# A decoder layer with a state-space mixer: local outputs and states in two phases over both row halves, later gate tiles in other PSUM banks, carried factors made on GpSimd

## The reference, cut to what matters

```python
zxbcdt = X @ W_in.T
z, xBC, dt = jnp.split(zxbcdt, [D_INNER, D_INNER + CONV_DIM], axis=-1)
dt = jax.nn.softplus(dt + dt_bias)
...                                   # causal convolution of 4 taps over xBC, then silu
x, Bm, Cm = jnp.split(xBC, [D_INNER, D_INNER + D_STATE], axis=-1)
dA = jnp.exp(dt * A)                  # 16 heads of 64 channels, 64 states
dBx = jnp.einsum('blh,bln,blhp->blhpn', dt, Bm, xh)
def step(h, inp):
    h = h * dA_t[:, :, None, None] + dBx_t
    y = jnp.einsum('bhpn,bn->bhp', h, C_t)
...
y = ys.transpose(1, 0, 2, 3) + D[None, None, :, None] * xh
y = y * jax.nn.silu(z)
y = y * jax.lax.rsqrt(jnp.mean(y * y, axis=-1, keepdims=True) + EPS) * norm_w
return y @ W_out.T
```

## Time and profile before

| | us |
|---|---|
| median of 3 runs | 2098.51 (2094.14 to 2098.99) |
| the profiled execution | 2095.91 |
| its span | 2094.1 |
| the mixer, from the start to the first matmul of the next stage | 911 |
| one sequence of it, the sixth (582.20 to 689.47) | 107.27 |
| its four groups and its tail | 17.05, 17.69, 17.09, 12.55, 42.88 |
| TensorE busy, of the span | 1952.8 (93%) |

### The profile page before, as it was taken

The page is one execution under the profiler, slowest core; times in us unless marked ns, Lnnn a source line. Parts: engine busy times, 40 slices in busy tenths (PEclk is TensorE's granted clock), DMA queues, the critical chain, the costliest instruction groups (busy, mean ns, idle before and its releaser), DMA issues. The chain is left out here.

```text
span 2094.1 us, 38522 instructions
## 1 busy us (share of the span) xinstructions
PE 1952.8 (93%) x12588; PEld 1310.0 (63%) x12588; DVE 1453.7 (69%) x2889; ACT 1223.2 (58%) x3068; POOL 410.5 (20%) x629
## 2 busy tenths in 40 slices
PE   7899999999999999858999999999999999889988
PEld 5667676767676767535565566555565655478853
DVE  8978787878787878525757676757676766555438
ACT  4435353444444453316878787877878686646514
POOL 1110111111111010230122222221313122200006
PEclk9999999999999999889999999999999999999999
DMA  7121222222221212232334333332323332641156
GB/s 217 49 76 63 61 79 60 79 50 89 50 89 42 97 34 85 81 114 62 102 82 122 82 111 83 106 92 90 109 88 100 104 87 77 192 162 61 61 178 265
DMA packets 120044, 200.60 MB, mean 96 GB/s; under 512 B 23088, under 2 KB 44592, under 8 KB 119600
## 3 DMA queue, kind: packets, MB, share of 16 engines
q1 hardware_dynamic: 110640, 179.20, 28.2%
q0 software_dynamic: 9216, 18.89, 3.5%
HBM read 117.27 MB, written 29.88 MB: 70 GB/s over the span
## 5 line engine op out<-in xcount | busy, mean ns | idle before, releaser
L1777 ACT ACTIVATE a_shared<-a_shared,a_mx 128x512 f32<-128x512 f32 x512 | 341.4, 670 | 62.8 <-DVE a_mx L1838 62.7
L1770 ACT ACTIVATE a_probs<-a_scores 128x512 f32<-128x512 f32 x512 | 292.3, 605 | 92.0 <-PE a_scores L1980 89.7
L1838 DVE TENSOR_REDUCE a_mx<-a_shared 128x1 f32<-128x512 f32 x512 | 318.8, 683 | 17.4 <-PE a_shared L1964 16.4
L1980 PE MATMUL a_scores<-a_qs,a_ks 98*128 98x512 f32 x512 | 217.7, 433 | 23.5 <-ACT a_probs L1770 20.0
L1964 PE MATMUL a_shared<-a_ks,a_qs 96*128 96x512 f32 x512 | 215.8, 432 | 24.6 <-ACT a_shared L1777 14.9
L939 PE MATMUL m_proj<-m_xt_hi,link 128*128 128x512 f32 x544 | 223.7, 411 | 6.8 <-DVE m_acc L652 6.8
L1094 PE MATMUL m_outp<-m_wout,m_g 128*128 128x512 f32 x512 | 226.0, 600 | 2.7 <-issue 2.7
L940 PE MATMUL m_proj<-m_xt_lo,link 128*128 128x512 f32 x544 | 214.7, 395 | 0.0
L941 PE MATMUL m_proj<-m_xt_hi,link 128*128 128x512 f32 x544 | 213.5, 392 | 0.0
L467 ACT ACTIVATE m_acc<-m_proj,m_cb,m_cw 128x512 f32<-128x512 f32 x72 | 58.1, 817 | 257.8 <-PE m_proj L941 257.6
L1938 PE MATMUL a_shared<-link 128*128 128x512 f32 x768 | 189.7, 400 | 18.6 <-POOL a_ks L1700 15.8
(11 more groups left out here) (267 smaller groups left out, 3456.4 us busy)
## 6 DMA issues: line engine op xcount, KB each, us to landing
m_dec<-step_decay SPq DMA_DIRECT2D x64, 256.0 KB, 4.1
a_qs<-link SPq DMA_DIRECT2D x256, 64.0 KB, 2.5
m_ce<-run_decay SPq DMA_DIRECT2D x128, 112.0 KB, 3.6
a_ks<-a_k_hi POOLq DMA_DIRECT2D x192, 64.0 KB, 2.5
e_x<-x SPq DMA_DIRECT2D x11, 1024.0 KB, 5.7
m_xt_in<-x_t_in SPq DMA_DIRECT2D x8, 1024.0 KB, 7.4
m_x_tok<-x_in SPq DMA_DIRECT2D x8, 1024.0 KB, 5.7
x<-m_x_tok SPq DMA_DIRECT2D x32, 256.0 KB, 2.2
```

The lines of the kernel that those rows point to most:

```text
L1770: act.activation(probs[:, n % 2, h, :], scores[t.score_bank(n, h)][:, :], ACT.Exp, scale=-1.0).then_inc(exp_ready, 1)
L1777: act.activation(scored[:, :], scored[:, :], ACT.Exp, scale=-1.0, bias=mx[:, i % 2, j, h:h + 1], accum_out=den[:, i, j, h:h + 1]).then_inc ...
L1838: dve.tensor_reduce(mx[:, i % 2, j, h:h + 1], bank(what)[:, :], AX.X, ALU.min).then_inc(mx_ready, 1)
L1980: pe.matmul(scores[t.score_bank(n, h)][:, :], ks[0:STACK + 2, t.slot(i), h, j * P:(j + 1) * P], qs[0:STACK + 2, t.slot(i), h, :], start=Tr ...
```

## The change

Five things change, all in the mixer.

1. The local outputs are written in two phases. In phase 0 row half 0 writes into y bank 0 and row half 1 into y bank 1, in phase 1 the other way round, and the products of both row halves alternate. The number of products is the same (32 of the program for each group; a product of two fp32 operands shows as two records in the trace). Phase 0 stands where the local outputs stood, phase 1 behind the first part of the added states.
2. The added states are split likewise: chunks 0, 5 and 2, then 4, 1, 6 and 3. The semaphore `half_done` stands in place of `even_done`.
3. From group 1 on the first gate tile goes to `outp` 1 and the second to `proj` 0, and the second y bank of group 3 is `outp` 1. With this go other waits: the first gate tile no longer waits for a convolution, the local outputs of group 3 wait for only one of the two skip terms, and each half of `xdt` is waited for by itself.
4. The carried factors are made by GpSimd, one group ahead of its sums of squares, and no longer by VectorE.
5. The decays of group 3 are made half in group 0 and half in group 1 (two heads each), and ahead of the states. In the first sequence they stay where they were.

```diff
+        def z_bank(gr, j):
+            return proj[j] if gr == 0 else (outp[1], proj[0])[j]
+
+        def y_bank(gr, j):
+            return outp[1] if gr + 1 == NG and j else yp[j]
...
+        STATE_PHASES = [(0, 5, 2), (4, 1, 6, 3)]
...
+            def carried_factors(b, gr):
+                loaded = value(pool, at(b, 64 * NG // 2, 64 * (gr // 2 + 1)))
...
+                pool.wait_ge(ce_in[gr % 2], loaded)
+                pool.tensor_tensor(ce[:, gr % 2], ce[:, gr % 2],
+                                   ct[:, Q:SEQ].unsqueeze(1).to_broadcast([P, 2, SEQ - Q]), ALU.mult
+                                   ).then_inc(ce_ready, 1)
...
                 for gr in range(NG):
-                    sum_squares(b, first, gr)
+                    carried_factors(b, gr)
+                    if gr:
+                        sum_squares(b, first, gr - 1)
+                sum_squares(b, first, NG - 1)
...
-            def local_decays(b, gr):
+            def local_decays(b, gr, heads=range(HG)):
...
-            def carried_factors(b, gr):
-                dve.wait_ge(ce_in[gr % 2], at(b, 64 * NG // 2, 64 * (gr // 2 + 1)))
-                dve.tensor_tensor(ce[:, gr % 2], ce[:, gr % 2],
...
-                        carried_factors(b, gr)
+                    if not first and gr < 2:
+                        local_decays(b, NG - 1, range(2 * gr, 2 * gr + 2))
                     states(b, first, gr)
                     if first and gr + 1 < NG:
                         local_decays(b, 1 + gr)
-                    elif gr == 0:
-                        local_decays(b, NG - 1)
...
-                elif (n - 2) % 4 < 2:
-                    pe.wait_ge(z_ready, at(b, XT_TILES, 2 * ((n - 2) // 4 - 1) + (n - 2) % 4 + 1))
+                elif part >= 2 and gr == 0:
+                    pe.wait_ge(conv_read, at(b, 9, part))
+                elif part == 2:
+                    if gr >= 2:
+                        pe.wait_ge(z_ready, at(b, XT_TILES, 2 * gr - 1))
+                    elif not first:
+                        pe.wait_ge(out_read, at(b, TT, 0))
+                elif part == 3:
+                    pe.wait_ge(conv_read, at(b, 9, 2 * gr + 2))
+                elif part == 0:
+                    pe.wait_ge(z_ready, at(b, XT_TILES, 1 if gr == 1 else 2 * gr))
...
-                for c in (0, 2, 4, 6, 1, 3, 5):
+                if phase == 0:
...
+                    pe.wait_ge(xw_ready, weighted)
+                else:
...
+                    pe.wait_ge(half_done, halves)
+                for c in STATE_PHASES[phase]:
...
-                for r in range(2):
-                    half = slice(r * Q, (r + 1) * Q)
-                    for j in range(2):
...
+                for k in range(CH):
+                    if phase == 0 and k % 2 == 0:
+                        met(pe, w_used, 1)
+                        pe.wait_ge(xdt_ready, scaled[k // 2])
+                    for h in range(2):
+                        for r in range(2):
+                            j, half = r ^ phase, slice(r * Q, (r + 1) * Q)
+                            ins = pe.matmul(y_bank(gr, j)[h * HP:(h + 1) * HP, k * P + r * Q:k * P + (r + 1) * Q],
+                                            xdt[half, k, 2 * j + h, :], dec[half, gr, 2 * j + h, k * Q:(k + 1) * Q],
+                                            start=(phase == 0 and k == 0), stop=False, skip_group_check=True)
...
-                    local_outputs(b, first, gr)
+                    local_outputs(b, first, gr, 0)
                     if gr + 1 < NG:
                         z_tile(b, first, gr + 1, 0)
                     elif more:
                         dt_proj(b + 1, False)
-                    added_states(b, first, gr)
+                    added_states(b, gr, 0)
+                    local_outputs(b, first, gr, 1)
+                    added_states(b, gr, 1)
```

100 lines of the change are left out of this document (49 added, 51 removed).

## The result

| | before | after | ratio |
|---|---|---|---|
| median us (range, runs) | 2098.75 (2094.14 to 2100.26, 4) | 2136.08 (2134.93 to 2137.55, 4) | 1.0184 [1.0168, 1.0200] |
| span of the profiled execution | 2094.1 | 2135.8 | |

A forecast was written before the change was run, and what follows sets the result against it. TensorE was taken to set the mixer's pace, VectorE close behind. Six middle sequences (-9.9), the last (-1.65) and the first (-2) sum to -13.6 us, -11.8 with the clock: median 2086 us, range 2075 to 2101.

The forecast's parts named there:

- the one on GpSimd: GpSimd's new carried-factor products: 2.2 us each, fitting its idle time, costing VectorE 0.4 us in the second group.
- A forecast of +0.5: First group of a middle sequence: early decays delay the states, so it ends 0.5 us later; bounds 0.3 to 0.7.
- The second group: Second group: 17.69 to 17.1 us, gain 0.6; scans go first at the port after the last sum, costing 0.4.
- GpSimd is first at the port: Rival, second group: carried factors start before the scans, which stand 2.2 us, 1.8 more in seven groups: 2099; chance 0.15.
- a rival of 0.10: Clock rival: half clock after the first group's wait, 1.7 us per x-tile stretch, last groups too: 2101 to 2113; chance 0.10.
- the forecast's two: Last groups: half clock expected in two more of seven, +1.8 us in all; bounds -2.6 to +3.6.
- the first sequence: First sequence: VectorE loses carried factors but GpSimd blocks its casts and splits; 2 us shorter, bounds -4 to 0.
- a forecast gain of 11.8: Whole kernel: all sequences sum to -13.6 us, -11.8 with the clock's loss in last groups.
- The two blocks: TensorE's local outputs and states per group: blocks of 0.71 and 1.46 us, 2.17 in place of 3.53.
- the row halves' overlap: TensorE's blocks: row halves run side by side; the rival without overlap keeps 3.53 us, total 2098, chance 0.08.
- The last group: Last group of a sequence: only the second block counts, 0.15 us less; the step-size tile still waits for the split.
- The sum: Whole kernel: profiled execution 2095.91 becomes 2084 us; median said as 2086.

The follow-up runs named there:

- e2: The kernel before with only the carried factors moved to GpSimd, in the changed kernel's order: 2138.0 us, 1.0183 of before.
- e9: The changed kernel with only GpSimd's first two products moved, behind the scaled x and group 0's first state: 2116.0 us, 1.0097 of before.
- e3: The changed kernel with GpSimd's products delayed: first until x is scaled, second until group 0's first state, third until group 3's decays: 2090.8 us, 0.9965 of before.
- e6: The changed kernel with each GpSimd product for the carried factors cut into four of 224 elements, same queue place: 2111.1 us, 1.0046 of before.
- e7: The changed kernel with only GpSimd's third product moved, behind the decays of group 3: 2114.5 us, 1.0057 of before.
- e5: The changed kernel with nine unused matmuls before the second group's carried outputs, from the second sequence on: 2143.4 us, 1.0198 of before.
- e8: e3 with the early decays moved between the two convolutions and no wait for GpSimd's third product: 2063.6 us, 0.9813 of before.
- e10: e8 with the carried factors on VectorE, ahead of the states: 2086.9 us, 0.9951 of before.
- e4: The changed kernel with factors on VectorE and group 3's decays behind group 0's states, leaving phases, banks and waits: 2090.2 us, 0.9960 of before.

## Why the prediction was wrong

**The step that failed** is the one on GpSimd: "Four of them fit into GpSimd's idle time", "nothing waits for them. What they cost is VectorE's", and that cost was set at 0.4 us, in the second group alone. I had the mechanism, with its rows, and applied it only to the place where I had moved the scans. I did not ask what VectorE does when the first two products start. They are released by B and C's turn and their loads, and stand ahead of all sums, right behind the power that the normalization waits for, so they run beside the normalization of the sequence before: 5.58 - 1.92 = 3.66 us, seven times. A forecast of +0.5 became +4.0. e2 shows it by itself, e9 and e3 remove it, e6 takes most of it by the size of the instruction alone. That GpSimd's own busy share was 20% spoke for nothing.

One sign of it was in my own rows and I misread it. The prediction says that the cast and the carried factors both agree with the rule on instructions with two inputs in SBUF, and lists scans, products and gates as those that can be caught. But the cast reads one tile (`m_dec`), and it stood all the same; so does the normalization's `tensor_scalar`.

**The second group** was the other miss: "I take them to be [...] and to go first", since VectorE asks first, at a cost of 0.4. VectorE did go first, with its first scan, which stood only for the last sum (0.96 us for 0.66). What failed is that I took the two scans as one piece of work. They are two instructions, and GpSimd's product, which waited for the first scan (2.51 for 2.12), had its turn between them; the second scan stood it out, 2.54 us. The price is that of the rival "GpSimd is first at the port": 18.77 here against 16.90 in e3 and e7 is 1.87, and the rival had 1.8. Its mechanism, the product ahead of both scans, is not what the rows show, so its price was right in part by luck.

The Trainium skill, "SBUF — State Buffer", section "Who interferes with whom", says that whoever issues first holds the shared ports for the whole instruction and the other fully blocks, and counts `tensor_scalar` and `cast` among those that can take the pair. By that rule the first group should have been checked too; the runs agree with it (1.92 to 5.58 beside GpSimd's 4.37, and 2.68 when that is cut in pieces). In the stretches read here (the changed kernel and e6) the port changes hands after each instruction: GpSimd never had two in a row while VectorE waited.

**The clock** was sized wrong. The prediction held a wait of 1.9 us harmless by two stretches without matmuls at full clock, and priced half clock on x tiles at 1.7 us a stretch in a rival of 0.10. With the wait of the second group at 2.6 us in place of e3's 0.8 it came in every sequence from the second on: 17.30 against 15.70, and e5 removed just this. In e3, where the waits before the carried outputs are 1.4 and 0.8 us, no second or third group fell. For the last groups the same rival added 3.6 to the forecast's two; at 0.9 each and three there already, two more were left, 1.8. Measured, they gave none: 92.62 against 92.83.

Set against the profiled execution of e3, the mixer is 52.9 us longer, and that comes out of these two causes, since the first sequence (+1.4) and the last groups (-1.3) cancel: the port 3.63 and 1.87 in each of seven sequences, 38.5; the clock 11.2 in the third groups and 3.1 in the second groups of sequences 2 and 6. The sign does not hang on the clock: 38.5 against a forecast gain of 11.8.

**What held.** The two blocks (0.63 and 1.49 for 0.71 and 1.46), hence the row halves' overlap. The three groups 17.46, 16.90, 15.70 (forecast 17.5, 17.1, 15.7), once the port is out of the way, and with them the point that the first group gives its gain back to the decays in VectorE's chain: e8 moves them and has 15.70. In the second group the scans waited 0.28 us for the last sum of squares in e3 (1.54 for 1.26), forecast 0.4. The last group went from 12.55 to 12.46 at full clock (forecast 0.15 less): the split for which it waits began 3.8 us into it, as before (440.05 here, 422.46 in the earlier trace rows). The sum, 2084 for the profiled execution, was 2086.1 in e3's, and e3's median 2090.8 against the 2086 said. The product on GpSimd took 2.1 us alone, forecast 2.2, and 2.5 in the company of the scans.

**Open.** Why e5's step decays land later; which groups the clock falls in from run to run (the last one above all); and the first sequence, forecast 2 us shorter and up to 2.7 us longer than before with the factors on either engine. In the changed kernel its first and second groups have a granted clock of 0.91 and 0.92, before 1.00; no run parts that from VectorE's share. And why, in the last group, a wait of 1.9 us has half clock beside it in some sequences and not in others.

## What to carry to other kernels

Before moving an operation to an engine that is idle, list what the other engines do at the moment when it will start, not where it is used; two operations that shut each other out cost time even if both engines look free, and an instruction of the busy engine can stand for one whole instruction of the other each time. If it must run there, give it a wait that sends it beside work that does not mind, or cut it in pieces. And the place where a busy engine already waits (here 1.6 to 2 us ahead of each second convolution) was worth as much here (27 us, e8 against e3) as the place on another engine (23 us, e8 against e10).

## What the runs showed of the hardware

- GpSimd's product of two tiles of SBUF stops VectorE's `tensor_scalar` on 128x512 fp32 and its scans of 256 elements, but not its convolution taps, which read PSUM and SBUF: 1.92 to 5.58, 1.26 to 3.42, and 2.32 to 2.30 us. VectorE's products of two tiles of SBUF stand too (0.73 to 1.64 for two in e6).
- The two engines take turns by instruction. Beside two products in a row on GpSimd one VectorE instruction stood for the first and the next for the second (1.87 and 1.78 us); beside pieces a quarter as long two instructions stood 0.41 and 0.35. The waiting goes both ways: GpSimd's product took 2.51 us in place of 2.12 when a scan was ahead of it.
- A stretch of 3.4 us at half clock costs 1.6 us on x tiles (17.30 less 15.70), and nothing where another engine sets the end. In the first three groups such falls came in or behind waits of TensorE of 1.4 to 3.3 us for the states or the scaled x, with narrow products around them, but not behind each: a wait of 1.4 had one in one sequence of e9 and none in e3, and a wait of 2.6 had none in two sequences of e9. None came behind the waits of 0.4 to 0.8 us before the carried outputs in e3 and e4. Nine unused matmuls in one such wait removed the fall behind it in all seven sequences, and other falls came in its place.
- GpSimd needs 1.28 us for 512 elements of an fp32 product and 2.12 for 896.
